# Selective scan plus windowed attention on one core: four states a tile turned by TensorE in place of three

## What is computed

```python
dt = softplus(einsum('blr,dr->bld', dt, dt_w) + dt_b)
A = -exp(A_log)
def step(h, inp):
    dt_t, B_t, C_t, x_t = inp
    dA = exp(dt_t[:, :, None] * A[None])
    dBx = (dt_t * x_t)[:, :, None] * B_t[:, None, :]
    h = dA * h + dBx
    y_t = einsum('bdn,bn->bd', h, C_t)
    return (h, y_t)
y = ys + xc * D
y = y * silu(z)
out = einsum('bld,cd->blc', y, out_proj_w)
```

## Time and profile before

| | us |
|---|---|
| median of 3 runs | 6579.67 (6577.32 to 6579.70) |
| the profiled execution | 6579.83 |
| its span, first to last instruction | 6577.7 |
| scan stage within the span | 155 to 5362 |
| attention stage | 5362 to the end |

### The profile page before, as it was taken

One profiled execution on the slowest core, in us unless ns is written; L12 is line 12 of the kernel. 1 busy time (PEld: TensorE's weight loads), 2 busy tenths in 40 slices (PEclk: granted clock), 3 DMA queues, 4 the chain that ended last, 5 costly groups with the idle time before them and its releaser, 6 DMA issues. The chain is left out here.

```text
span 6577.7 us, 105792 instructions
## 1 busy us (share of the span) xinstructions
PE 6067.4 (92%) x35452; PEld 3884.7 (59%) x35452; DVE 5924.9 (90%) x7357; ACT 5010.0 (76%) x10458; POOL 5105.1 (78%) x4137
## 2 busy tenths in 40 slices
PE   7999999999999999999999999999999869999998
PEld 3555555555555555555555555555555557777776
DVE  6999999999999999999999999999999976666666
ACT  3888888888888888888888888888888854343443
POOL 2999999999999999999999999999999961010100
PEclk8999999999999999999999999999999989999999
DMA  6222222222222222222222222222222312222222
GB/s 262 102 100 100 100 100 100 100 100 100 100 101 100 101 100 100 100 100 102 102 101 100 100 100 100 100 100 100 100 100 100 119 43 71 84 84 81 91 74 72
DMA packets 175235, 656.80 MB, mean 100 GB/s; under 512 B 28044, under 2 KB 28268, under 8 KB 149860
## 3 DMA queue, kind: packets, MB, share of 16 engines
q1 hardware_dynamic: 174692, 650.05, 26.9%
HBM read 477.19 MB, written 153.88 MB: 96 GB/s over the span
## 5 line engine op out<-in xcount | busy, mean ns | idle before, releaser
L967 POOL TENSOR_TENSOR dbx<-u,bb 128x512 f32<-128x512 f32 x3072 | 3836.1, 1276 | 261.5 <-DVE h L811 210.4
L801 DVE TENSOR_TENSOR_SCAN p_da<-p_da,state_v,dbx 128x512 f32<-128x512 f32 x1728 | 2165.3, 1274 | 0.8 <-ACT p_da L627 0.6
L627 ACT ACTIVATE p_da<-dt,neg_a 128x512 f32<-128x512 f32 x3072 | 2091.0, 692 | 72.5 <-DVE h L811 27.0
L811 DVE TENSOR_TENSOR_SCAN h<-p_da,state_h,dbx 128x512 f32<-128x512 f32 x1344 | 1703.8, 1275 | 138.1 <-ACT p_da L627 106.4
L1108 PEld LDWEIGHTS p_yt<-ident,hc_v 128*128 128x128 f32 x6912 | 872.0, 146 | 803.4 <-issue 644.8
L820 DVE TENSOR_TENSOR hc_v<-cc,p_da 128x512 f32<-128x512 f32 x1728 | 1144.5, 672 | 24.0 <-PE p_yt L1108 20.4
L1037 PE MATMUL p_g<-xs,win 128*128 128x512 f32 x2304 | 1155.6, 599 | 3.8 <-DVE xs L770 3.4
L1108 PE MATMUL p_yt<-ident,hc_v 128*128 128x128 f32 x6912 | 1074.7, 283 | 87.0 <-DVE hc_v L820 85.4
L976 POOL TENSOR_TENSOR hc_g<-h,cc 128x512 f32<-128x512 f32 x768 | 978.2, 1274 | 0.0
L1033 PE MATMUL p_g<-xb,cdiag 128*128 128x512 f32 x1536 | 766.0, 595 | 1.9 <-ACT halo L573 1.9
L661 ACT ACTIVATE hct<-p_yt,ct 128x128 f32<-128x128 f32 x2304 | 655.7, 373 | 44.5 <-PE p_yt L1147 44.5
(11 more groups left out here) (163 smaller groups left out, 8580.0 us busy)
## 6 DMA issues: line engine op xcount, KB each, us to landing
bb<-bc_spill SPq DMA_DIRECT2D x128, 1024.0 KB, 10.1
cc<-bc_spill SPq DMA_DIRECT2D x64, 1024.0 KB, 8.0
xc_spill<-xc SPq DMA_DIRECT2D x96, 512.0 KB, 2.6
z_spill<-zt SPq DMA_DIRECT2D x96, 512.0 KB, 3.9
xj<-xc_spill SPq DMA_DIRECT2D x192, 256.0 KB, 4.1
zj<-z_spill SPq DMA_DIRECT2D x192, 256.0 KB, 2.7
cc<-x SPq DMA_DIRECT2D x48, 768.0 KB, 5.9
xc<-in_x SPq DMA_DIRECT2D x33, 768.0 KB, 10.7
```

What stands on the lines that cost most here:

```text
L627: nc.scalar.activation(p_da[n % RD][:], dt[:, d % 2, :], ACT.Exp, scale=neg_a[:, d, n:n + 1])\
L801: nc.vector.tensor_tensor_scan(psum, psum, dbx[:, n % RB, :], state_v[:, d, k:k + 1], ALU.mult, ALU.add).then_inc(s_scan, 1)
L811: nc.vector.tensor_tensor_scan(h[:, k, :], psum, dbx[:, n % RB, :], state_h[:, d, k:k + 1], ALU.mult, ALU.add).then_inc(s_scan, 1)
L967: nc.gpsimd.tensor_tensor(dbx[:, n % RB, :], u[:, d % 2, :], bb[:, n, :], ALU.mult)\
```

## The change

One state goes from `BY_DVE` to `BY_TURN` and two swap places: `BY_POOL` is now (0, 5, 6, 13), `BY_TURN` (3, 4, 7, 11), and the rest, 1, 2, 8, 9, 10, 12, 14 and 15, are `BY_DVE`. `h` and `hct` grow by one slot, and one row of C less is loaded into `cc`. Beside that the tables of slots are new.

```diff
-BY_POOL = (0, 5, 6, 12)
-BY_TURN = (4, 7, 11)
+BY_POOL = (0, 5, 6, 13)
+BY_TURN = (3, 4, 7, 11)
...
-TURN_STATE_AT, TIMES_CT_AT, KEEP_AT = (8, 9, 13), (8, 12, 14), 13
-LAG, LAG_V, LAG_G = 4, 2, 6
+TURN_STATE_AT, TIMES_CT_AT, KEEP_AT = (8, 10, 12, 14), (8, 10, 12, 14), 13
+LAG, LAG_V, LAG_G = 3, 3, 2
...
-MEAN_AT, CENTRE_AT, SQUARE_AT = 4, (4, 7, 10), (3, 7, 9)
-VAR_AT, RSTD_AT, NORM_AT = 11, 10, (14, 15, 17)
-OUT_AT, OUT_SLOTS, RESIDUAL_AT = (7, 12, 18), (4, 4, 3), (11, 17, 24)
-IN_AT, IN_SLOTS = (22, 41, 59), (18, 18, 19)
-COPY_LATER, SILU_LATER = 0, (9, 6, 3)
-X_AT, COPY_X_AT, TURN_C_AT, COPY_CT_AT, SCALE_AT = (78, 80, 81), 82, 85, 86, (88, 89, 93)
+MEAN_AT, CENTRE_AT, SQUARE_AT = 2, (4, 6, 9), (2, 5, 8)
+VAR_AT, RSTD_AT, NORM_AT = 12, 10, (14, 15, 16)
+OUT_AT, OUT_SLOTS, RESIDUAL_AT = (7, 13, 18), (4, 4, 2), (12, 17, 21)
+IN_AT, IN_SLOTS = (21, 41, 59), (19, 18, 19)
+COPY_LATER, SILU_LATER = 0, (8, 4, 3)
+X_AT, COPY_X_AT, TURN_C_AT, COPY_CT_AT, SCALE_AT = (79, 81, 82), 84, 85, 89, (87, 88, 90)
...
-DT_AT, SOFTPLUS_AT, DT_X_AT = 6, 6, 12
+DT_AT, SOFTPLUS_AT, DT_X_AT = 6, 6, 10
```

## The result

The changed kernel takes 6549.95 us (median of 6 runs, 6545.47 to 6554.27), the kernel before 6578.49 beside it (6 runs, 6575.75 to 6580.77): a ratio of 0.9956 [0.9945, 0.9967], 28.5 us or 0.43% faster. The forecast was 6524 us, 56 us faster: the direction is right, the gain is half as large. The profiled execution took 6548.85 us, its span is 6546.7, against 6577.7 before.

A forecast was written before the change was run, and what follows sets the result against it. DVE was taken to set the pace almost everywhere, with the other engines close behind. Six tile terms gave 161.6 us a chunk, 53 us less in 31 chunks plus about 3 in the last: 6579.8 - 56 = 6524 us, range 6450 to 6605.

The forecast's parts named there:

- the six terms: Gate-to-gate times of a chunk's six tiles, together 161.6 us, 1.7 us less a chunk.
- d0 to d1: First to second gate of a chunk: DVE 30.25 us, PE 31.4 in half the chunks, mean 30.8.
- d5 to d0: Last gate to next chunk's first: one DVE product and the waits for the mean go, 25.1 us.
- d1 to d2: Second to third gate of a chunk: PE comes last with 26.2 us of work, taken as 26.1.
- d4 to d5: Fifth to sixth gate: ACT stays some 0.9 us late behind the third silu, product-slot wait goes, 25.7 us.
- d2 to d3: Third to fourth gate: PE, without a gap, sets it and gets 0.43 us more work; 26.4 us, 0.2 more.
- d3 to d4: Fourth to fifth gate: ACT sets it, shorter stretch and earlier silu cancel, DVE stops at state 3; 27.5 us as before.
- The last chunk: The chunk without input projection at the end: about 3 us less.
- DVE's waits: Sign in the scan stage: DVE busy down by 110 us, its waits up by some 50.
- That DVE's work sets the pace everywhere: Scan stage: PE's gaps absorb its added work, so the 113 us go; 6467, or 6431 with mean and residual; chance 0.2.
- The two slower ones: ACT becomes the bound between third and sixth gates, 6639 us, chance 0.12; PE's clock falls more often, 6633, chance 0.08.
- The second, that gains are eaten up: Mean still late or gates wait for longer turning back, and ACT costs the rest: 6567 to 6590 us, chance 0.16.

The follow-up runs named there:

- the parts alone: Two kernels: only the new sets and turn slots in the kernel before, 6684.15 us; the old sets and turn slots in the changed kernel, 6604.31 us.

## Why the prediction was right, and where it failed

- **The method held in size.** Read from gate to gate, each of the six terms is within 0.5 us of its measured mean. Measured less forecast they are, from d0 to d1 on, 0.17 - 0.17 + 0.24 + 0.18 + 0.49 - 0.02 = 0.9, the distance from 161.6 to 162.5. The chunk of before is 163.5 by the mean of all gates and not 163.3, 0.2 the other way, so the gain was 1.7 - 0.9 + 0.2 = 1.0 a chunk. Of 113 us of DVE time saved, 29 arrived; the prediction had let 56 through.
- **d5 to d0** (25.1, measured 25.08): right, both DVE's product and the mean. **d0 to d1** (30.8, measured 30.97): right. Without a wait it is 30.25 and with the lower clock 31.40, as worked out; there were 19 such chunks in place of 15. The mean alone gave 11 us where its waits were 27, since in that kernel five chunks had a clock of 0.89 or 0.90 from d0 to d1, and L786 waited 11 us longer there.
- **d1 to d2** (26.1, measured 25.93): right in size, **the owner not shown**. The gate waits 1.04 us for the turning back, as expected of a tile where PE comes last, but with 0.43 us less PE work it stays at 25.7 or 26.1, by the clock of the interval before, and neither 0.75 us less ACT work nor 0.39 more DVE work moves its mean by more than 0.1. So the 0.43 that the prediction added to PE's 25.8 is not what gives this interval its length, and the value was met in part by luck.
- **d4 to d5** (25.7, measured 26.19) is **the term that was mis-sized most**, 0.5 x 31 = 15 us. The step "ACT is late by some 0.9 us behind the third silu, as now" put the stop too low, and the same tile's wait at the gate at nothing: DVE's work is 24.65 us, the stop 1.11 and the gate waits 0.39, together 26.15. "As now" can't be read from the waits, either. In the kernel before, DVE's only listed wait between these gates is the 0.66 us for the product slot, with ACT's lateness hidden behind it (DVE, then ACT, of the kernel before):

```profile
2728.36 0.69 DVE L820 TENSOR_TENSOR hc_v<-cc,p_da 128x512 f32<-128x512 f32 x1 [0.66 <-PE p_yt L1108]
2728.97 2.51 DVE L811 TENSOR_TENSOR_SCAN h<-p_da,state_h,dbx 128x512 f32<-128x512 f32 x2
```

```profile
2728.15 0.69 ACT L627 ACTIVATE p_da<-dt,neg_a 128x512 f32<-128x512 f32 x1
```

  That exponential ends at 2728.84, 0.13 before the scan that reads it. So the wait for the slot did go, as forecast, but without it DVE would have stood there for ACT, by these rows 2728.84 - (2728.97 - 0.66) = 0.53 us (an estimate), and only a small part of the 0.66 was to be won.
- **d2 to d3** (26.4, measured 26.64): the size nearly right, **the owner wrong**. "PE without a gap" does not mean that PE needs the time. The relief of PE left it at 26.63 (PE waited for ACT in its place), and with less ACT work at slot 14 the same 129 matmuls pass through in 25.92, where they were shown as 26.41 busy.
- **d3 to d4** (27.5, measured 27.68): the place was right, with DVE's stop at the scan of state 3. The times worked out came close: ACT's stretch from the first silu's end to the second's start is 2844.20 - 2822.76 = 21.44 us (forecast 21.7; 2822.76 is 1.29 behind the start of the table load back at 2821.47), and the second silu starts 16.81 behind the gate of d3 (forecast 17.0). But "ACT, not DVE, sets this tile", by its stretch of work between the silus, is the reason that fell. 0.75 us of ACT work less at slot 8 is worth 0.00; 0.75 at slot 14 is worth 0.65; 0.39 us more on DVE behind the stop costs 0.40. What sets it is the way round: DVE's work from a stop to slot 12, PE's turning there, ACT's chain of 10.4 us, the scan. That 27.5 was nearly met, although the reason given for it fell, is in part luck.
- **The last chunk** was forecast at -3 us and came at +1.5, another 4.5 us.
- **DVE's waits** were to rise by some 50 us. The four kinds that changed most went from 106.4 + 27.1 + 20.4 + 12.1 = 166 us to 200.6 + 43.0 = 244, so by 78. A wait at the gate was expected in d2 and d3; it came in d2 and d5.
- **The rivals.** That DVE's work sets the pace everywhere is excluded by d2 to d5. The two slower ones did not come, with d3 to d4 under 28 and the clock at 1.00 from d1 to d5. The second, that gains are eaten up, describes the missing half: the waits grow by what DVE saves.
- **What failed as a whole** is the pricing of waits and of spare work taken from the kernel before: the amount of work on one engine, or a wait in front of another. The runs with the parts alone (+106 and +26 us) show that prices taken one by one do not add up here.

Still open: which of the new slots bring the 134 us; what sets d1 to d2 (25.73 to 25.99 us in all kernels with the new sets and tables but those with the last turn at 13); and why the clock from d0 to d1 is 1.00 in some chunks and 0.95 or 0.90 in others. No run takes work from POOL, which is busy for 25.30 of 26.07 us in d1 to d2 and for 26.19 of 26.19 in d4 to d5. It is not what holds d4 to d5, since DVE waits there for ACT and PE and the interval falls to 25.48 with less ACT work; for d1 to d2 it is a rival that is not tested.

## What to carry to other kernels

Where engines run in order and hand work round, look for the way round (stop, work, hand-over, chain, stop), and price an edit by its place on it: 0.75 us of the same work was worth nothing on one side of a hand-over and 26 us in total on the other, and one added product was free ahead of a stop and paid in full behind it. A busy engine without gaps is no proof that it is the bound; only taking work from it is. A new split of work between engines and the slots of that work belong together, so tune them together and don't judge either alone; and before work goes to another engine, ask whose stream is ahead at that slot.

## What the runs showed of the chip

- A wait can hide under a short instruction's shown length: the `keep_state` is shown as 0.20 us, and the `times_ct` behind it can start 0.05 after its start (slot 14) but starts 0.28 after it at slot 12, and 0.06 with less PE work. About 0.23 us of waiting at slot 12 is in no list of waits.
- A wait can also hide behind another one: where the wait for a product slot went, one for ACT stood behind it.
- ACT's switch of function tables is 1.28 us shown, and the next ACTIVATE starts 1.29 us behind its start (2844.20 to 2845.49), so no further cost shows beside it.
- Four transposes more a tile did not lower the granted clock in the scan stage: 0.96 before, 0.97 after. In d0 to d1, behind the tile at 0.79, it did differ from chunk to chunk (1.00, 0.95, 0.90), and that alone moves a chunk by up to 2.8 us.
